# Second network's feed-forward layer norms on turned tiles with GpSimd, and one branched padding place on TensorE

## What is computed

```python
def _layer(x, wqkv, qs, ksc, wo, lg, lb, w1, b1, w2, b2):
    ...
    x = x + o @ wo
    h = shift_token(x)
    mu = h.mean(-1, keepdims=True)
    var = h.var(-1, keepdims=True)
    h = (h - mu) / jnp.sqrt(var + 1e-05) * lg + lb
    h = h @ w1 + b1
    a, g = jnp.split(h, 2, axis=-1)
    h = a * jax.nn.gelu(g, approximate=False)
    x = x + h @ w2 + b2
    return x
```

## Time and profile before

| | us |
|---|---|
| median of 3 runs | 2202.27 |
| lowest and highest | 2198.31, 2203.32 |
| the profiled execution | 2202.99 |
| its span, first to last instruction | 2201.2 |

### The profile page before, as it was taken

How to read it: one execution, slowest core, us unless ns; L and a number is a source line. 1 busy time by engine, 2 the same in 40 slices (tenths; PEclk the granted TensorE clock), 3 DMA queues, 4 the chain that set the end, 5 groups by cost and what they waited for, 6 DMA issues and landing times. The chain is left out here.

```text
span 2201.2 us, 90075 instructions
## 1 busy us (share of the span) xinstructions
PE 2082.7 (95%) x33646; PEld 1433.0 (65%) x33646; DVE 1822.4 (83%) x4873; ACT 1682.5 (76%) x5850; POOL 1390.0 (63%) x1318
## 2 busy tenths in 40 slices
PE   7989999999999999999999999999998887899997
PEld 5656666666666666666666666666666664666665
DVE  5888888888888888888888889888886588888873
ACT  4767888888888888888888888888887335788784
POOL 1337777777776777777676777767674125666660
PEclk9999999999999999999999999999999998999999
DMA  4001222112211222112221122112211100000001
GB/s 117 5 3 36 73 61 50 42 51 68 59 46 43 67 61 52 44 46 74 61 49 44 51 66 61 45 45 56 54 49 39 31 17 6 14 16 11 16 6 29
DMA packets 144806, 97.03 MB, mean 44 GB/s; under 512 B 61977, under 2 KB 137409, under 8 KB 144385
## 3 DMA queue, kind: packets, MB, share of 16 engines
q1 hardware_dynamic: 143232, 91.02, 16.3%
q10 hardware_dynamic: 1152, 0.26, 0.1%
HBM read 23.11 MB, written 1.05 MB: 11 GB/s over the span
## 5 line engine op out<-in xcount | busy, mean ns | idle before, releaser
L739 PE MATMUL bank<-wqkv,hs 128*128 128x512 f32 x1344 | 658.8, 610 | 4.9 <-ACT arena L1595 2.5
L1983 POOL TENSOR_TENSOR arena<-arena,rnorm 128x512 f32<-128x512 f32 x448 | 455.5, 1046 | 281.8 <-DVE rnorm L259 280.6
L1976 POOL TENSOR_TENSOR arena<-arena 128x512 f32<-128x512 f32 x448 | 567.0, 1276 | 57.8 <-DVE arena L2196 57.6
L1624 ACT ACTIVATE arena<-bank,amx 128x64 f32<-128x64 f32 x1536 | 459.0, 337 | 14.3 <-DVE amx L2247 14.1
L1624 ACT ACTIVATION_READ_ACCUMULATOR arena<-bank,amx 128x1 f32 x1536 | 354.0, 230 | 0.0
L739 PEld LDWEIGHTS bank<-wqkv,hs 128*128 128x128 f32 x1344 | 229.8, 191 | 177.9 <-issue 157.7
L2191 DVE TENSOR_TENSOR arena<-bank,rot 128x512 f32<-128x512 f32 x448 | 306.4, 684 | 35.5 <-PE bank L739 33.5
L760 PEld LDWEIGHTS bank<-ident,arena 128*128 128x128 f32 x1792 | 211.5, 141 | 188.2 <-issue 116.9
L2196 DVE TENSOR_TENSOR arena<-bank,rot 128x256 f32<-128x256 f32 x896 | 333.2, 413 | 0.0
L1601 ACT ACTIVATE arena<-bank 128x512 f32<-128x512 f32 x426 | 252.1, 628 | 102.2 <-PE bank L760 102.1
L1990 POOL TENSOR_TENSOR arena<-arena,ainv 128x512 f32<-128x512 f32 x192 | 200.5, 1044 | 195.2 <-DVE ainv L2255 195.2
(11 more groups left out here) (226 smaller groups left out, 3306.2 us busy)
## 6 DMA issues: line engine op xcount, KB each, us to landing
arena<-arena SPq DMA_DIRECT2D x768, 64.0 KB
wqkv<-in_L_ffn_Wqkv_dram SPq DMA_DIRECT2D x24, 256.0 KB
hs<-z SPq DMA_DIRECT2D x128, 32.0 KB, 1.8
hs<-z SPq DMA_DIRECT2D x128, 31.8 KB, 1.9
fx<-z SPq DMA_DIRECT2D x31, 128.0 KB, 2.2
fx<-z SPq DMA_DIRECT2D x31, 127.0 KB, 2.5
wqkv<-in_L_ffn_Wqkv_dram SPq DMA_DIRECT2D x24, 128.0 KB
w<-in_L_ffn_W_dram SPq DMA_DIRECT2D x6, 341.0 KB
```

The lines of the kernel that those rows point to most:

```text
L739: nc.tensor.matmul(bank[o][:], src[:], wqkv[w][:, off:off + 512], start=True, stop=True).then_inc(AT[name] if part < 2 else AT[name][i], 1)
L1624: ins = nc.scalar.activation(pb[i][0][p % 2][:, h * DH:(h + 1) * DH], bank[3 + g][:, j * DH:(j + 1) * DH], ACT.Exp, bias=amx[p % 2][:, i, ...
L1976: nc.gpsimd.tensor_tensor(t, t, rs[i][c], ALU.add).then_inc(AT["ak" if c else "aq"][i], 1)
L1983: nc.gpsimd.tensor_tensor(t, t, rnorm[p % 2][:, i, HU * c:HU * c + HU].unsqueeze(2).to_broadcast([P, HU, DH]), ALU.mult).then_inc(AT["mk" ...
```

## The change

In the second network, groups 24 to 30 take the form that the first network has: `ff_mean`, `ff_var`, `ff_broadcast` on PE, `ff_centre` and `ff_normalise` on DVE and `ff_square` on ACT go; `ff_tokens` and `ff_channels` on PE (slots 0 and 3), `ff_tokens` on ACT (in the place of `ff_square`), `ff_stats` and `ff_aggregate` on DVE (slot 1, ahead of `ff_close`) and `ff_normalise` on POOL (after division (1, s-2, 1), ahead of the add of unit 1's queries) come. `ff_affine` reads PSUM in both networks. Group 31, in the tail, keeps its form. The two padding places at even steps go; one comes at odd steps ahead of the turned keys of unit 0, slot 60, with `max_nops=0`: a branch over the padding in place of NOPs.

```diff
--- before.py
+++ after.py
@@ -30,7 +30,7 @@
 NSQ = 9
 P0, P1, P2 = 4.997384728560895, -3.334408639284136, 0.3755197794197683
 NLAYER = 8
-FETCH_BLOCK, KEYS_AT, OUTPUTS_AT = 256, 62, {0: 254, 2: 251}
+FETCH_BLOCK, SCORES_AT = 256, 60
 
 
 def rotary_constants(window):
@@ -544,7 +544,7 @@
                 else:
                     for i in range(2):
                         sp.wait_ge(AT["res"][i], nth(i, ph["lo"] + 2 * g + 1))
-                at(sp, FF["in"] if ph["net"] == 0 else FF["tok"], f)
+                at(sp, FF["in"], f)
                 b = 4 * (g % 4)
                 sp.dma_start(fx[0:DH, :, :], zb[0:DH, b:b + 4, :]).then_inc(FF["x"], 16)
                 sp.dma_start(fx[DH:P, :, 1:P], zb[DH:P, b:b + 4, 0:P - 1]).then_inc(FF["x"], 16)
@@ -854,8 +854,8 @@
                     mm.then_inc(AT["y"][name], 1)
 
                 def ff_tokens(f):
-                    if f == 0:
-                        pe.wait_ge(LN["xn"], NBLK + 4)
+                    if f == 4 * ph["layer0"]:
+                        pe.wait_ge(LN["xn"], NBLK + (4 if ni == 0 else 12))
                     at(pe, FF["hid"], 3 * f)
                     pe.wait_ge(FF["x"], 32 * (f + 1))
                     for j in range(4):
@@ -867,27 +867,6 @@
                     pe.wait_ge(FF["xn"], 2 * f + 2)
                     for j in range(4):
                         mm = nc.tensor.transpose(bank4[2][:, j, :], ftok[:, j, :], ident[:])
-                    mm.then_inc(FF["bc"], 1)
-
-                def ff_mean(f, s):
-                    if f == 4 * ph["layer0"]:
-                        pe.wait_ge(LN["xn"], NBLK + 12)
-                    at(pe, FF["hid"], 3 * f)
-                    pe.wait_ge(FF["x"], 32 * (f + 1))
-                    nc.tensor.matmul(bank[2][:], mean_w[:], fx_f, start=True, stop=True).then_inc(FF["in"], 1)
-
-                def ff_var(f):
-                    at(pe, FF["z"], f)
-                    pe.wait_ge(FF["st"], f + 1)
-                    for j in range(4):
-                        mm = nc.tensor.matmul(bank[2][:, 2 * j:2 * j + 2], fsq[:, j * P:(j + 1) * P], mean_w[:, 0:2],
-                                              start=True, stop=True)
-                    mm.then_inc(FF["mv"], 1)
-
-                def ff_broadcast(f, s):
-                    pe.wait_ge(FF["rstd"], NSQ * (f + 1))
-                    for j in range(4):
-                        mm = nc.tensor.transpose(bank4[2][:, j, :], fy[2][:, j:j + 1].to_broadcast([P, P]), ident[:])
                     mm.then_inc(FF["bc"], 1)
 
                 def ff_gate(f, c, s):
@@ -968,13 +947,11 @@
                         group_norm_1(s, slot_)
                     c, f, before = ff_phase(ph, s)
                     if c == 0 and f >= 0 and slot_ == 0:
-                        ff_mean(f, s)
+                        ff_tokens(f)
                     if c == 0 and before >= 0 and slot_ == 1:
                         ff_down(before, s)
-                    if c == 0 and f >= 0 and slot_ == 2:
-                        ff_var(f)
                     if c == 0 and f >= 0 and slot_ == 3:
-                        ff_broadcast(f, s)
+                        ff_channels(f)
                     if c == 0 and f >= 0 and slot_ == 4:
                         ff_gate(f, 0, s)
                     if c == 1 and f >= 0 and slot_ < 2:
@@ -1031,14 +1008,12 @@
                         keys(1, s)
                         at(pe, AT["sqq"], un(0, s))
                         queries(1, s)
-                    if live(s - 7) and live(s) and s % 2 == 0:
-                        pe.addr_align(FETCH_BLOCK, offset=OUTPUTS_AT[s % 4])
                     if live(s - 3):
                         at(pe, AT["oe"][1], s - 2)
                         project_out(s - 3, (0, 1), 0)
                     feed_forward_0(s, 1)
-                    if live(s - 3) and live(s - 1) and s % 2 == 0:
-                        pe.addr_align(FETCH_BLOCK, offset=KEYS_AT)
+                    if live(s - 3) and live(s - 1) and s % 2:
+                        pe.addr_align(FETCH_BLOCK, offset=SCORES_AT, max_nops=0)
                     if s == hi:
                         pe.wait_ge(AT["sqq"], un(1, hi - 1))
                         pe.wait_ge(AT["sqk"], un(1, hi - 1))
@@ -1662,20 +1637,12 @@
                     at(act, FF["bc"], f)
                     nc.scalar.activation(fcen, bank[2][:], ACT.Copy).then_inc(FF["tok"], 1)
 
-                def ff_square(f):
-                    act.wait_ge(FF["tok"], f + 1)
-                    at(act, FF["mv"], f)
-                    nc.scalar.activation(fsq, fcen, ACT.Square).then_inc(FF["st"], 1)
-
                 def ff_affine(f):
                     if f % 4 == 0:
                         act.wait_ge(ld_ff, 192 * (f // 4 + 1))
-                    if ni == 0:
-                        act.wait_ge(FF["bc"], f + 1)
-                    else:
-                        act.wait_ge(FF["xn"], f + 25)
+                    act.wait_ge(FF["bc"], f + 1)
                     w = f // 4 % 2
-                    nc.scalar.activation(fxn, bank[2][:] if ni == 0 else fxn, ACT.Identity, scale=lnp[w][:, 0:1], bias=lnp[w][:, 1:2]
+                    nc.scalar.activation(fxn, bank[2][:], ACT.Identity, scale=lnp[w][:, 0:1], bias=lnp[w][:, 1:2]
                                          ).then_inc(FF["aff"], 1)
 
                 def ff_gelu(f):
@@ -1745,7 +1712,7 @@
                         n = 10 + (s - lo - 1) // 2
                         g_square(act, n, n - 8)
                     if c == 0 and f >= 0:
-                        ff_square(f)
+                        ff_tokens(f)
                     if live(s):
                         square(0, s, 1)
                     if live(s - 2):
@@ -1834,7 +1801,7 @@
 
             def half_affine(h):
 
-                act.wait_ge(FF["xn"], 56 + h)
+                act.wait_ge(FF["xn"], 63 + h)
                 nc.scalar.activation(half(fxn, h), half(fxn, h), ACT.Identity, scale=lnp[1][:, 0:1], bias=lnp[1][:, 1:2]
                                      ).then_inc(FF["aff"], 1)
 
@@ -2041,6 +2008,9 @@
                         normal(1, s - 1, 1)
                     if live(s - 2):
                         divide(1, s - 2, 1)
+                    c, f, before = ff_phase(ph, s)
+                    if c == 0 and f >= 0:
+                        ff_normalise(f)
                     if live(s - 1):
                         add(1, s - 1, 0)
                         normal(1, s - 1, 0)
@@ -2277,24 +2247,15 @@
                         ins = nc.vector.bn_aggr(f_mv[:, j, :], f_st[:, j, :])
                     ins.then_inc(FF["mv"], 1)
 
-                def ff_centre(f):
-                    dve.wait_ge(FF["in"], f + 1)
-                    nc.vector.tensor_tensor(fcen, fx_f, bank[2][:], ALU.subtract).then_inc(FF["tok"], 1)
-
                 def ff_newton(f):
                     for k in range(NSQ):
                         if k == 0:
                             dve.wait_ge(FF["mv"], f + 1)
-                            var = f_mv[:, :, 1] if ni == 0 else bank[2][:, 0:8].rearrange("p (b a) -> p b a", a=2)[:, :, 0]
-                            ins = nc.vector.tensor_scalar(f_s, var, EPS, None, ALU.add)
+                            ins = nc.vector.tensor_scalar(f_s, f_mv[:, :, 1], EPS, None, ALU.add)
                         else:
                             dve.wait_ge(FF["rstd"], NSQ * f + k)
                             ins = inverse_root(k, f_s, f_b, f_c, fy[0][:], fy[1][:], fy[2][:])
                         ins.then_inc(FF["rstd"], 1)
-
-                def ff_normalise(f):
-                    dve.wait_ge(FF["bc"], f + 1)
-                    nc.vector.tensor_tensor(fxn, fcen, bank[2][:], ALU.mult).then_inc(FF["xn"], 1)
 
                 def ff_gate(f, c):
                     w = CH[c][1]
@@ -2360,14 +2321,13 @@
                     if s - lo in (1, 3):
                         group_norm_1(s, slot_)
                     c, f, before = ff_phase(ph, s)
-                    if c == 0 and f >= 0 and slot_ == 0:
-                        ff_centre(f)
+                    if c == 0 and f >= 0 and slot_ == 1:
+                        ff_stats(f)
+                        ff_aggregate(f)
                     if c == 0 and before >= 0 and slot_ == 1:
                         ff_close(before)
                     if c == 0 and f >= 0 and slot_ == 2:
                         ff_newton(f)
-                    if c == 0 and f >= 0 and slot_ == 3:
-                        ff_normalise(f)
                     if c == 0 and f >= 0 and slot_ == 4:
                         ff_gate(f, 0)
                     if c == 1 and f >= 0 and slot_ < 2:
```

## The result

The changed kernel took 2226.74 us (median of 4 runs, 2225.03 to 2228.87), the kernel before 2202.33 us beside it (2198.31 to 2203.32): a ratio of 1.0112, with a 95% interval of 1.0094 to 1.013, so it is slower by 1.1%, 24.4 us. The forecast was 2226 us. The profiled execution of the changed kernel took 2228.87 us, its span is 2227.0 us; it was the longest of its four, so the two traces are 25.8 us apart where the medians are 24.4. Lines have moved: `ff_tokens` is L862 (was L877), `ff_channels` L869 (L890), the gate matmul L878 (L899), ff_down L894 (L915), ScalarE's copy L1638 and affine L1645 (L1678), GpSimd's add L1943 (L1976), normal L1950 (L1983) and norm L1963 and L1966, VectorE's root L2254 to L259 (L2289).

The account below looks back on a forecast made before the run. TensorE's own work bounds the first network; in the second, what delays TensorE's odd step delays everything after. Norms +27.1 and padding -4.2 make +22.9 on 2203.0, about 2226 us; 8-in-10 range 2206 to 2244.

Parts of the forecast that it names:

- Steps 1 to 7 of the norms: Second network, one odd-even pair: chain from the token transposes through copy, root and GpSimd to the gate matmul, +4.5 us.
- step 2: Second network, odd step: ff_down waits for ScalarE's copy, which stands behind the turned keys and queries; +1.9 us.
- step 7: Second network: GpSimd's add, queued behind the norm, delays VectorE's rotation by 4.8 us and the gate matmul by 4.5.
- The padding: First network: removing NOPs gives back the issue waits before L852 and L760, -4.2 us, bounds 0 and 7.
- Rival D: First network: the branch costs 0.6 us at 47 places, 28 us on top, 2254 us; chance 0.08.
- The 39 to 51 slots: First network, odd steps: instruction slots of 1280 the branch skips at each of 47 places, target in the same block.
- Rival E: First network: padding not jumped over, NOPs exceed 1.8 us of cover, 24 x 1.3 = 31 us, 2257; chance 0.03.
- The end: Group 30, last with the new norms: no next rotation, GpSimd's delay alone and a shorter hold, +2.0 us.
- group 24: First group of the second network's new norms: no ff_down before it, so 4.5 - 1.9 = +2.6 us.
- Rivals A: Second network: the second hold, for root and GpSimd's norm, hides or rotation doesn't bind; +5, 2208 us; chance 0.08.
- Rival B: TensorE the only bound, copy and turned tile early: 0.7 us saved per group plus 4.2 padding, 2194 us; chance 0.05.
- C: About even: holds fall into TensorE's 9 us of idle time in the second network, padding gives 7; 2203 +- 4; chance 0.04.

Follow-up runs that it names:

- e5: Changed kernel with ScalarE's copy of the turned tokens ahead of unit 1's second-half exponents, VectorE's root left in place; 2207.7 us, ratio 1.002.
- e6: Changed kernel with GpSimd's add and normal of unit 1's queries moved ahead of the norm's two passes; 2217.7 us, ratio 1.0059.
- e3: Changed kernel with VectorE's root moved from slot 2 to slot 1, right behind the statistics; 2212.0 us, ratio 1.0033.
- e10: Changed kernel with ScalarE's copy early and GpSimd's add and normal ahead of the norm, TensorE's order untouched; 2211.5 us, ratio 1.0028.
- e4: e3 with ScalarE's copy of the turned tokens also moved ahead of unit 1's second-half exponents; 2219.8 us, ratio 1.0069.
- e1: Kernel before with only the padding edit, old norms kept; 2193.2 us, ratio 0.995.
- e8: e1 with the new single padding place filled with NOPs instead of jumped over by a branch; 2217.1 us.
- e11: Kernel before with no padding at all, neither NOPs nor branch; 2261.8 us.
- e2: Only the norm edit: changed kernel with the two old NOP places put back and the branch taken out; 2237.9 us, ratio 1.015.
- e7: e10 with TensorE's four transposes back moved behind unit 1's projections of keys and values; 2193.3 us, ratio 0.9949.

## Why the prediction was right, and where it was not

**Steps 1 to 7 of the norms** are there one by one, with 1.90 us (forecast 1.9) ahead of ff_down, 1.74 us (1.75) for the root, 2.39 us from the root's end to the transposes back (2.5), a rotation held by the add, and +4.5 us in the group where the clock stays up. e5 takes step 2 away and e6 step 7; the pair moves by 2.2 (beside the clock) and 1.0 us, against 1.9 and 0.9.

**The missing term is TensorE's clock.** The prediction gave TensorE's holds their length and nothing more. In four of five groups the clock fell behind them for 3.4 us and cost 1.5 to 1.7 us, 6.6 us in all. It was a term to bound: the earlier trace rows show 1.00 for a TensorE that is nearly always busy, and the plan put two idle stretches of 2 us into each pair. Which hold is followed by it is left open: the one of 1.9 us has none behind it when the other is gone (e3), the one of 1.7 us has none when the first is gone (e5), one of 2.3 us had it once in the groups of e10, those of 2.7 (e6) and 3.9 us (e3) in group 24 have it, and e4's of 3.1 us in every group.

**The padding** was forecast at -4.2 us from waits of the first network only. The waits were read in a stretch that ends at 1680 us; the largest of that kind stands at 1688 us, 4.2 us with the clock behind it, and one of 1.44 us at 214. By itself the padding is worth -11.7 us (e1); in the changed kernel, by its trace, 5.2 us up to group 24. Rival D is refuted: the branch lasts some 0.3 us and is covered. The 39 to 51 slots hold, within one, at 46 places; the first has 160. Rival E's condition did not arise; NOPs in that place do cost (e8), but its sum of 24 x 1.3 us is not how they cost it: 6.9 us for the short holds, 15.4 at the first place. Leaving the edge where it falls (e11) was the larger danger, 68.6 us, and the prediction had no rival for it.

**The end** was forecast at +2.0 us and gave +0.2, and group 24 +1.9 for 2.6. The kernel before has a half-clock record at 2182.7 us in its last stage that the changed one hasn't, and e2, with the same norms, has two (2200.6, 2217.7) and is 3.4 us longer than the kernel before from the tokens of group 30 on. So the clock has a part in this term too, and none was forecast.

So the mechanism was right and the closeness of 2226 us is in part luck: the norms were under-rated by some 6 us (27.1, where e2 has 33) and the padding by some 7 (4.2, where e1 has 11.7), and the two errors cancel. Rivals A, B and C are refuted: the second hold didn't hide, the copy didn't come early. Rival B's condition, both holds away, is nearly what e7 sets up by other moves, and its 2193.3 us lie by B's 2194; but B had 0.7 us gained in each group and 4.2 by the padding, and e7 has 0.4 lost in each pair and the padding's 11.7.

## What to carry to other kernels

Before an operation is handed to an engine that is idle on average, follow its result to the engine that sets the end, and look there for work that needs nothing of it: four passes moved ahead of the transposes hid 1.7 us of every hold, and with the copy and the add moved as well the same new norms went from +33 us to nothing. What is moved takes its place in two orders, that of its engine's queue (e4: a residual behind a root) and that of its neighbour in time (e4, e10: VectorE beside GpSimd); both have to be read off the timeline. Price an idle stretch that is put into a busy TensorE at more than its length, and when a kind of wait is summed up, sum it over the whole run, the first and the last padded place included.

## What the runs showed of the hardware

- At holds of about 2 us TensorE's granted clock was at half for 3.4 us, from 0.3 us before to 1.2 us after work had begun again, in four of five groups of the changed kernel; 3.1 us of wait brought 3.4 or 6.8 us of it (e4), 9.4 us of wait 13.7 us (e8).
- VectorE's operations of 128x4 elements take 0.16 us alone; beside passes of GpSimd on 128x512 they took 0.38 to 0.96 us and ended with the pass (e3, e4, e10). The Trainium skill, SBUF — State Buffer, section Who interferes with whom, names the port pair that the two engines share as the only cause of contention; here it fits the root's 3.9 us in e4 and the 0.6 us more of wait in e10.
- The place of TensorE's instructions modulo 256 is worth 68.6 us in a kernel of 2200 (e11 against e1). The waits, most of them inside a group of 48 short matmuls and up to 2.4 us there, all stand at the edge of a block of 256 slots.
- A NOP took 75 ns on TensorE's sequencer (160 in 12 us, e8). A branch over 38 to 51 slots took some 0.3 us there, the one over 160 slots into the next block 1.78 us (e1), and neither held up the matmuls.
